# A recommender's interaction layer: pairs and dense rows turned two units later, the gram two units sooner, layer 2's activation ahead of the copies, and the first pair's lookups in six PSUM banks

## The reference

```
e = stack([tbl_f[ids[:, f]] for f in range(26)], axis=1)   # 2048 x 26 x 128
v = concatenate([dense[:, None, :], e], axis=1)            # 2048 x 27 x 128
g = einsum('bnd,bmd->bnm', v, v)                           # every pair of the 27 vectors
z = concatenate([dense, g[:, upper triangle]], axis=1)     # 128 + 351
h = relu(concatenate([z, dense], axis=1) @ W1 + b1)        # 607 -> 512
h = relu(h @ W2 + b2)                                      # 512 -> 256
y = h @ W3                                                 # 256 -> 1
```

## Time and profile before

| | |
|---|---|
| Median of 3 runs | 452.38 us (450.32 to 454.48) |
| Profiled execution | 455.76 us, span 453.8 us, mean granted TensorE clock 0.947 |
| TensorE matmul, busy | 377.8 us, 83% |
| TensorE weight load, busy | 341.5 us, 75% |
| VectorE | 254.9 us, 56% |
| ScalarE | 146.3 us, 32% |
| GpSimd | 231.0 us, 51% |
| DMA | 36.37 MB, 80 GB/s; its share falls from 9 tenths in the first 57 us to between 1 and 5 |

### The profile page before, as it was taken

How to read it: one execution, slowest core, us unless ns; L and a number is a source line. 1 busy time by engine, 2 the same in 40 slices (tenths; PEclk the granted TensorE clock), 3 DMA queues, 4 the chain that set the end, 5 groups by cost and what they waited for, 6 DMA issues and landing times.

```text
span 453.8 us, 14936 instructions
## 1 busy us (share of the span) xinstructions
PE 377.8 (83%) x6224; PEld 341.5 (75%) x6224; DVE 254.9 (56%) x767; ACT 146.3 (32%) x265; POOL 231.0 (51%) x244
## 2 busy tenths in 40 slices
PE   0769993968989799887998789887999788998877
PEld 0758893967887688876897689776998687886645
DVE  5997798663534865456555766456654765321110
ACT  2355130413313342333323342332413351335212
POOL 4365656465465454556555555555565535556000
PEclk9998996878996999999899999999998998999969
DMA  7999925151431314132341517151343411111000
GB/s 182 230 225 231 241 60 105 34 103 46 80 77 49 83 40 104 40 83 68 60 84 45 99 41 85 60 102 49 66 90 53 86 29 40 40 40 48 4 1 0
DMA packets 25441, 36.37 MB, mean 80 GB/s; under 512 B 5378, under 2 KB 19594, under 8 KB 25417
## 3 DMA queue, kind: packets, MB, share of 16 engines
q1 hardware_dynamic: 17577, 20.27, 24.6%
q0 software_dynamic: 7680, 15.74, 12.9%
q10 hardware_dynamic: 160, 0.01, 0.0%
HBM read 35.99 MB, written 0.01 MB: 79 GB/s over the span
## 4 chain that ended last, share of the span: by engine, by line
PE 69%; DVE 12%; issue 11%; DMA 3%; POOL 2%; ACT 1%; SPq 0%; DVEq 0%; ACTq 0%
PE hid L421 11%; DVE onehot L607 9%; PE look_ps L379 8%; PE look_ps L377 8%; PE gram L449 8%; PE look_odd L379 6%; PE hid L428 6%; PE look_odd L377 6%; PE vec_act L332 5%; POOL vecs L315 2%; DMA vecs<-tbl,ids_sb 2%; PE hid L377 2%; PE hid L379 2%; PE look_odd L374 2%; PE small L390 2%
## 5 line engine op out<-in xcount | busy, mean ns | idle before, releaser
L315 POOL DMA_INDIRECT vecs<-tbl,ids_sb x240 | 230.8, 962 | 187.0 <-issue 121.0
L607 DVE TENSOR_SCALAR onehot<-step_ids,row_no 125x256 fp32r<-125x256 int32 x704 | 210.6, 361 | 141.4 <-PE look_ps L379 49.0
L377 PE MATMUL look_ps<-onehot,look_hi 125*128 125x256 f32 x312 | 85.1, 305 | 7.8 <-DVE onehot L607 3.9
L580 ACT COPY vecs_T<-vec_act 128x512 f32<-128x512 f32 x64 | 37.6, 597 | 151.7 <-remote 67.3
L379 PE MATMUL look_ps<-onehot,look_lo 125*128 125x256 f32 x312 | 80.6, 291 | 1.6 <-issue 1.6
L449 PE MATMUL gram<-vecs_T 128*27 128x26 f32 x4096 | 50.3, 197 | 22.6 <-issue 22.5
L377 PEld LDWEIGHTS look_ps<-onehot,look_hi 125*128 125x128 f32 x312 | 62.2, 199 | 8.6 <-issue 8.1
L449 PEld LDWEIGHTS gram<-vecs_T 128*27 128x27 f32 x4096 | 43.9, 108 | 31.4 <-issue 28.1
L377 PE MATMUL look_odd<-onehot,look_hi 125*128 125x256 f32 x240 | 63.8, 300 | 1.9 <-issue 1.8
L379 PEld LDWEIGHTS look_ps<-onehot,look_lo 125*128 125x128 f32 x312 | 62.2, 199 | 3.4 <-issue 3.2
L379 PE MATMUL look_odd<-onehot,look_lo 125*128 125x256 f32 x240 | 60.1, 284 | 2.8 <-issue 2.7
(11 more groups left out here) (89 smaller groups left out, 325.7 us busy)
## 6 DMA issues: line engine op xcount, KB each, us to landing
step_ids<-look_ids SPq DMA_DIRECT2D x7, 768.0 KB
table_raw<-tbl SPq DMA_DIRECT2D x11, 448.0 KB
step_ids<-look_ids SPq DMA_DIRECT2D x7, 640.0 KB
vecs<-tbl,ids_sb POOLq DMA_INDIRECT x240
step_ids<-look_ids SPq DMA_DIRECT2D x11, 128.0 KB, 10.8
vecs<-dense SPq DMA_DIRECT2D x16, 64.0 KB
table_raw<-tbl SPq DMA_DIRECT2D x11, 52.0 KB
w_sb<-w SPq DMA_DIRECT2D x1, 512.0 KB
```

The lines of the kernel that those rows point to most:

```text
L315: nc.gpsimd.indirect_dma_start(out=vecs[j][:, 1 + k, :], out_offset=None, in_=tables[k], in_offset=bass.IndirectOffsetOnAxis(ap=ids_sb[:, ...
L377: nc.tensor.matmul(bank, look_hi[:, f, ch, :], onehot[:, SLOT[g], c, :], start=ch == 0, stop=False)
L580: return engine_copy(vecs_T[j][:, :, 1 + lo:1 + hi], bank[:, 0:hi - lo, :].rearrange("d v b -> d b v"))
L607: last = nc.vector.tensor_scalar(onehot[:, SLOT[g], c, :], step_ids[a][0:LOOK_K, f - TABLES_OF[a][0], :], row_no[0:LOOK_K, ch:ch + 1], Non ...
```

## The change

In every tile TensorE turns the dense rows and the folded pairs after unit 3 instead of after unit 1. VectorE folds the gram of the tile before after four units, not after six or five. ScalarE merges and takes its first duo ahead of the pairs and the dense rows, and does `relu2` before group 2's copy instead of after group 3's. One-hot compares take float ids and a constant; ScalarE subtracts each partition's first row number from the ids in place (`shift_ids`), table by table in the first pair, then once per half pair; VectorE waits for that, and SyncE issues one more load at the end. In the first pair six duos have six banks (`look_first`, two of them the gram's, whose memsets go, one `small`), TensorE turns tile 0's halves at units 10 and 18, ScalarE casts eight tables ahead, and TensorE waits for tile 2's first gathered rows before the second half of tile 0's gram, as well as for tile 0's copies before the last duo.

```diff
 looked_late = sb("looked_late", [D, LOOKUPS - EARLY, P])
-row_no = sb("row_no", [P, LOOK_CH])
+row_first = sb("row_first", [P, 1])
...
 vec_banks = [bank[:, :, :].rearrange("p v b -> p (v b)") for bank in vec_act]
+look_first = [hid1_bank, look_ps[0], look_ps[1], gram_banks[:, 0:512], gram_banks[:, 512:1024], small[:, :]]
...
 gathered = [[sem(f"gathered{j}_{h}") for h in range(2)] for j in range(2)]
+ids_shifted = sem("ids_shifted")
...
 
-FIRST_TURN, SECOND_TURN = 6, 4
+FIRST_TURN, SECOND_TURN = 10, 6
...
 
-        def load_step(a, pair):
+        def load_step(a, pair, cols=None):
...
             sp.wait_ge(onehot_made, unit_count(pair - 1, 2 * hi - 1))
-            src = look_ids[lo:hi, bass.ds(pair * PAIR, PAIR)]
+            src = look_ids[lo:hi, bass.ds((pair if cols is None else cols) * PAIR, PAIR)]
...
             load_dense(2 * r + 1, 1)
+
+        load_step(0, pairs, pairs - 1)
...
                 pe.wait_ge(y_copied, pair)
+            if isinstance(t, int) and t == 1:
+                pe.wait_ge(looked_up, DUOS)
...
             duo = f // 2
-            bank = look_ps[DUO_BANK[duo]][:, f % 2 * PAIR:(f % 2 + 1) * PAIR]
-            plain = isinstance(pair, int) and pair == 0 and f >= PLAIN
+            first = isinstance(pair, int) and pair == 0
+            bank = (look_first[duo] if first else look_ps[DUO_BANK[duo]])[:, f % 2 * PAIR:(f % 2 + 1) * PAIR]
+            plain = first and f >= PLAIN
...
             pe.wait_ge(onehot_made, unit_count(pair, g))
-            if half == 0 and f % 2 == 0 and positive(DUOS * pair + duo + 1 - DUO_BACK[duo]):
+            if first and half == 0 and duo == DUOS - 1:
+                pe.wait_ge(dense_copied, 1)
+                pe.wait_ge(dense_placed, 1)
+            if half == 0 and f % 2 == 0 and not first:
...
             turn_group(n, k, 1)
+            unit(2)
+            unit(3)
...
                 pairs_out(t - 1)
-            for i in range(2, middle):
+            for i in range(4, middle):
...
                 unit(i)
+            if first:
+                rows_in(j, pair + 1, 0)
...
 
-        pe.wait_ge(ident_in, 16)
-        pe.wait_ge(dve_set, 3)
...
             if i == FIRST_TURN:
+                pe.wait_ge(ident_in, 16)
...
                 last = nc.vector.tensor_scalar(
-                    onehot[:, SLOT[g], c, :], step_ids[a][0:LOOK_K, f - TABLES_OF[a][0], :],
-                    row_no[0:LOOK_K, ch:ch + 1], None, ALU.is_equal)
+                    onehot[:, SLOT[g], c, :], step_ids[a][0:LOOK_K, f - TABLES_OF[a][0], :].bitcast(F32),
+                    float(ch), None, ALU.is_equal)
...
             if look:
-                dve.wait_ge(step_ids_in[j], 16 * (pair + 1))
-
-            middle = UNITS_OF[j] // 2
-            for i in range(middle):
+                dve.wait_ge(ids_shifted, LOOKUPS + t + 1)
+
+            for i in range(4):
...
                 turn(t - 1)
-            for i in range(middle, UNITS_OF[j]):
+            for i in range(4, UNITS_OF[j]):
...
 
-        nc.vector.memset(gram[:, 0:16, :], 0.0).then_inc(dve_set, 1)
-        nc.vector.memset(gram[:, 16:32, :], 0.0).then_inc(dve_set, 1)
-
         nc.vector.memset(pairs_T[96:P, CHUNKS - 1, :], 1.0).then_inc(dve_set, 1)
-        dve.wait_ge(row_no_in, 16)
...
                 if half == 0:
-                    dve.wait_ge(first_ids_in[f], 16)
+                    dve.wait_ge(ids_shifted, f + 1)
...
             lo = 2 * duo
-            bank = look_ps[DUO_BANK[duo]][:, 0:(f - lo + 1) * PAIR]
+            first = isinstance(pair, int) and pair == 0
+            bank = (look_first[duo] if first else look_ps[DUO_BANK[duo]])[:, 0:(f - lo + 1) * PAIR]
...
             act.wait_ge(onehot_used, unit_count(pair, g))
-            if isinstance(pair, int) and pair == 0:
+            if first:
...
 
+        def shift_ids(a, lo, hi):
+
+
+            rows = step_ids[a][0:LOOK_K, lo:hi, :]
+            nc.scalar.activation(rows.bitcast(F32), rows, ACT.Identity,
+                                 bias=row_first[0:LOOK_K, 0:1]).then_inc(ids_shifted, 1)
+
+        def shift_first(f):
+
+            a = f // FIRST_TABLES
+            act.wait_ge(first_ids_in[f], 16)
+            shift_ids(a, f - TABLES_OF[a][0], f - TABLES_OF[a][0] + 1)
+
+        def shift_step(a, pair):
+
+            act.wait_ge(step_ids_in[a], 16 * pair)
+            shift_ids(a, 0, TABLES_OF[a][1] - TABLES_OF[a][0])
+
...
                 move_dense(pair)
-            if not first:
-                copy_pairs(t - 1, 1 - j)
-            copy_dense(n, k, pair + j)
...
             unit(3)
+            if not first:
+                copy_pairs(t - 1, 1 - j)
+            copy_dense(n, k, pair + j)
+            if look:
+                shift_step(k, pair + 1 + j)
+            if mlp and j == 1:
+                relu2(pair - 1)
...
                 relu1(pair - 1, 0)
-            if mlp and j == 1:
-                relu2(pair - 1)
...
 
-        act.dma_start(row_no[:, :], row_numbers).then_inc(row_no_in, 16)
+        act.dma_start(row_first[:, :], row_numbers).then_inc(row_no_in, 16)
...
         act.sem_inc(y_copied, 1)
-        ahead = LOOKUPS // 2
+        ahead = PLAIN
+        act.wait_ge(row_no_in, 16)
+        shift_first(0)
...
             take_high(k)
+            shift_first(k + 1)
...
                     take_high(f + ahead)
+                if half == 1 and f + ahead + 1 < LOOKUPS:
+                    shift_first(f + ahead + 1)
+        shift_step(0, 1)
         tile(0, 0, 0, first=True, mlp=False)
-        act.wait_ge(dve_set, 3)
+        act.wait_ge(dve_set, 1)
...
 "identity": np.eye(P, dtype=np.float32),
-"row_numbers": np.arange(P * LOOK_CH, dtype=np.float32).reshape(P, LOOK_CH),
+"row_numbers": np.arange(0, -P * LOOK_CH, -LOOK_CH, dtype=np.float32).reshape(P, 1),
...
 arrays[f"tbl_{f}"] = np.ascontiguousarray(inputs[f"tbl_{f}"])
```

## The result

The changed kernel is slower: 466.68 us median of five runs (462.97 to 468.81) beside 452.81 (450.32 to 455.31) for the one before, ratio 1.0317, 95% interval 1.0271 to 1.0363. Its profiled execution took 462.97 us (span 461.0), the quickest of the five, where before's profiled 455.76 was 3 above its median: the two profiles show 7.2 us of the medians' 13.9.

The account below looks back on a forecast made before the run. GpSimd's gather bursts and the gaps between them were taken to bound the loop. First pair +9.8 and loop -3.6 gave +6.2: 462.0 us for the profiled execution, 458.5 against the median of 452.38; range 445 to 465.

Parts of the forecast that it names:

- +9.8 at the burst of 98.97: First pair: late shift, late rows and the new rows' wait delay this 8-gather burst to 108.8, +9.8 us.
- my 3.4: Second pair's first units: VectorE needs shifted ids, and that shift stands behind ScalarE's last duo copy, +3.4 us.
- the 2.4 "if the signal is held": First pair's end: if table 10's signal is held until 1.5 us after the gather burst, some 2.4 us more.
- my 4.8: First pair: the load of the next ids leaves 4.8 us later, since VectorE's twelve units run from 54.6 to 69.6.
- The rival of rows landing as before: Gathered rows in the first pair land when they did: +3.6 - 3.6, so 452.4 us; chance 0.06.
- The bound: Loop: GpSimd's bursts of 36.8 us plus four gaps of 3.03 allow no pair under about 48.9 us.
- I take -3.6: Loop: without the two waits, the gap ended by the even gram shrinks to 3.03 us, saving 3.6 over six rounds.
- The rest of the loop costs nothing in my sum: Loop: ScalarE's shifts (2.8 us a pair), VectorE's earlier folds and SP's extra load were counted as nothing.
- the clock goes: Rival, loop: TensorE's longer hold before each even gram costs it its clock, +3.6 us, 465.8; chance 0.12.
- the price of its rival: Rival, VectorE's compares: 194 ns, 99 less, taking 13.2 us off the kernel, to 445.4; chance 0.18.
- my 279: VectorE's compares: 279 ns each instead of 293, an effect taken as 0.
- The waits as the pace: Rival, loop: TensorE's two removed waits set the pace, so 11.8 us come off, 450.4; chance 0.20.

Follow-up runs that it names:

- the two later profiles of before: The unchanged earlier kernel profiled again on two other chips with bursts apart: 462.32 us (ratio 1.005) and 450.94 us (one run).
- the two placements: In the changed kernel's first pair, the wait for tile 2's rows and the first id shift behind the last two duo copies; undone: 454.38 us, 1.011 of before.
- Cutting the bursts: Kernel before with four of the eight gathers of each second half left out from tile 2 on, bursts apart: 419.77 us, 0.932 of before.
- d2_both: Changed kernel without the wait for tile 2's rows and with the first shift ahead of the last two duo copies, bursts apart: 454.38 us, 1.011 of before.
- b2_order: Kernel before with only the changed kernel's orders inside the tiles, bursts apart: 465.19 us, 1.012 of before.
- the d runs: Follow-up runs on one chip with bursts apart, where the kernel before took 451.41 us.
- both edits: To the changed kernel's first pair: no wait for tile 2's rows, first shift ahead of the last two duo copies; 1.011 of before apart, 1.027 joined.
- b4_constant: Kernel before with compares against a constant and ids read as float32, without the shift, bursts apart: 458.68 us, 0.996 of before.
- e1_same: Changed kernel timed and profiled again without edit, on a chip with joined bursts: 435.80 us, 1.063 of before.
- c1_few: Kernel before with four of the 15 gathers a tile left out from tile 2 on, joined bursts: 407.81 us, 0.980 of before.

## Why the prediction fell short

- **The direction and the first pair: right.** +9.8 at the burst of 98.97, measured +9.5, and 11.5 to 13.0 against the two later profiles of before. TensorE's idle ahead of the second pair came as 5.81 us, my 3.4 and the 2.4 "if the signal is held", which it was (7.50 us in front of the duo's copy). The load left 3.9 us later (my 4.8), the rows served a gram at 82.21 against my 82.7. The rival of rows landing as before is out. With the two placements undone 2.1% came back; how it divides between them was measured only with joined bursts (9 to 10 and 4 to 6 us).
- **The bound: right, and its size too kind.** Cutting the bursts took some 31 us off where they stand apart. But a pair still took 45.9 us then, only 4 to 5 under what GpSimd had allowed.
- **The loop: wrong. This is the step of the sum that failed: "I take -3.6", with "The rest of the loop costs nothing in my sum".** The first profiles have -1.1, and d2_both and b2_order against before's profile on their own chips have +1.4 and +2.3. By the ratio of the timed runs, d2_both is still 1.1%, 5 us, over before with the edits made. The gap that I had shrinking to 3.03 us measured 3.31, 4.15, 2.98, 3.88, 4.18 and 5.41, 23.9 in all against 24.9. In rounds 2, 4 and 5 the gram still started 2.4, 2.1 and 2.4 us after the burst's end, before 2.1, 2.3 and 2.3, and GpSimd 1.8 us after the gram instead of 1.55: TensorE had come sooner to its last units, but there it trickled. On the chip of the d runs, with both edits, 2.7 of my 3.6 did come; with the orders alone (b2_order) nothing. The gram's idle grew by 5.1 us in all, not by about 11.8.
- **What the sum had at nothing.** The bursts became 2.7 us longer with the new compares; I had taken their 36.8 us a pair as fixed. And the stretch behind the even gram, the rival "the clock goes", was 3.3 us longer in rounds 3 to 5 at 0.87 to 0.90, but 1.8 shorter in the other three: +1.5 in all, and +2.9 in d2_both (0.91 to 0.94 in rounds 2 to 5), near what before varies by itself; that rival had 3.6, with a chance of 0.12. The kernel before has such a clock in single rounds too (0.95 in rounds 1 and 3), and b4_constant, which has only the quicker compares, ran at 0.90, 0.93, 0.85, 0.94 and 0.99 in rounds 1 to 5: the orders alone are not shown to be its cause. Of the 3.2 us that the two other gaps gave in the first profiles, 2.2 stand in one round; they vary that much by themselves, so that the loop came out at -1.1 and not above 0 is luck.
- **The compare: the price of its rival came, its effect not.** 56 ns of 293 went. By the Trainium skill, VectorE: DVE Perf Modes, "The TRN2 errata", an estimate is 194 ns; the 237 measured here lie between that and my 279. VectorE's busy time fell by 41 us and at most 3.6 us followed, which b4_constant shows: the chain's 8.6% of compares was no price.
- **From the profile to the median.** The sum gave 462.0 for the profiled execution, which took 462.97. I then took off 3.4 us because before's profile stood that much above its median; after's stood 3.7 below its own. The step took how far one execution stood from its median for a term of the sum. In microseconds it is most of the miss: of the 8.2 us between 458.5 and 466.68, 7.1 stand here and 1.0 in the sum (loop +2.5, first pair -0.3, what follows the loop -1.2), so the sum's hit within 1 us is in part luck. Where these 7 us lie no profile shows: none of the slower executions was profiled, and e1_same ran with joined bursts. Some may be in the first pair, for which before's first profile was late by 2 to 3.5 us against the other two.
- **The waits as the pace** (rival, 0.20): out with bursts apart, by b2_order.
- **Open:** where the 22 to 25 us go with joined bursts. Both edits give back 11.6 to 13.3; the one wait of 11 us would about fill the rest, if the kernel before has none there. c1_few suggests it (in its loop the longest wait for rows is 0.95 us), but it has fewer gathers, and no profile of before shows it.

## What to carry to other kernels

A wait that lies under another engine's burst is not worth its length; ask what the waiting engine will do instead, and whether it can do that during the burst. A preparatory step (here a 1.56 us shift) costs what the instruction it is queued behind waits for: put it where its data are ready, not where its result is needed. When gathers and a large load share the DMA engines, the order in which they leave decides; a quicker engine that releases the load sooner can cost 11 us. How far one execution lies from its kernel's median is not a term of a sum.

## What the runs showed of the hardware

- The changed kernel ran in two ways by chip: 0.3 to 1.85 us between most gather bursts and 44.0 us a pair, or mostly 2.9 us and more, and 50 to 52. With bursts apart, TensorE late in a burst does 2 matmuls in 2 us, with idle time that no semaphore explains.
- An instruction that compares 256 float32 elements with a constant starts every 237 ns, with a per-partition operand and integer ids every 293. Beside the first form GpSimd's gathers take 988 to 992 ns in the mean, beside the second 959 to 965 (bursts apart).
- With joined bursts, a 768 KB load that leaves SyncE before the eighth gather of a tile's second half has ended is followed by 9.8 to 11.5 us of waiting for rows, 12 times of 12; one that leaves 0.3 us or more after it by 1.6 us at most.
- In every profile of the changed kernel and of the one before, one gather in the third round is followed by a pause of some 1.9 us (before: at 203.45 and 206.30); the changed kernel has it on both kinds of chip.
